# Second mixture's experts: plain scatters of half 1, the shared tiles moved behind all routed ones, and plain gathers into four pair buffers that VectorE adds to the rows

## The chip, the cores and the metric

The kernel runs on one core of one Trainium2 chip. The metric is the device time of one execution in microseconds (us), the median of several runs. Engines are called as in the profile: PE is TensorE, DVE VectorE, ACT ScalarE, POOL GpSimd, SP SyncE; SPq and POOLq are the DMA queues that SP and POOL fill.

## The reference, cut to what matters

Four layers run over 4096 rows of 128 numbers (16 sequences of 256): sparse attention, a mixture of experts, a state-space layer and a second mixture. The change lies in the last one:

```
scores = softmax(xf @ gate_w.T)
_, idx = top_k(scores + gate_b, 2)              # two of eight experts for each row
w      = take_along_axis(scores, idx)
expert(x, e) = silu((x@w1[e]+b1[e]) * (x@w3[e]+b3[e])) @ w2[e] + b2[e]
y = sum over the two chosen e of w * expert(x, e)
z = expert(x, shared)                            # every row also goes through a shared expert
out = x + y + z                                  # x: the rows that came in; y, z: of their normed copy
```

## The kernel before, in words

The 4096 rows are T = 32 tiles of 128 rows, in two halves of HT = 16 tiles. X (g_X in the profile) holds them in SBUF through all layers. For a mixture every row is sent to two slots, k = 0 and k = 1, of a buffer XG in HBM (rows in the profile), sorted by expert. Each half has NH = 39 tiles of slots, so NT = 78 routed tiles, and XG was zeroed at the program's start. POOL sends one tile of rows with one indirect DMA (`pool_scatter`, line 858); its argument op is ALU.bypass (a plain write) or ALU.add (the DMA reads the target, adds, writes). For each k the routing weight is first written beside the rows (`pool_reweight`, lines 846 to 854), which for k = 1 waits until the 16 scatters of k = 0 have landed. Half 0 of the second mixture is scattered by the state-space stage and by `dispatch` (lines 904 to 906, plain), half 1 by `experts` (lines 1106 to 1108, with add).

`experts` then runs one list of tiles, `sequence`, through a pipeline written out by hand. Each engine has a `step(s)` that handles tile s - lag: SP fetches tile s and stores tile s - 8; PE transposes tile s - 3 (m_x_TP, L1142), multiplies it up at s - 4 (m_x_UP, L1151), down at s - 6 (m_x_DP, L1171), and transposes the hidden values at s - 5 (m_x_HP, L1161); DVE adds the bias and multiplies the two parts at s - 4 (L1299, L1301) and takes the result at s - 6 (`output`); ACT copies out of PSUM between them. Routed tiles are fetched from XG (L1074), shared ones from the normed rows m_XS in SBUF (L1069). The list before has 110 places: routed tiles 0 to 38 (half 0), shared tiles 16 to 23, routed tiles 39 to 77 (half 1), shared tiles 0 to 15, shared tiles 24 to 31.

SP's fetch of a routed tile waits for `placed`, which POOL raises by 39 when a half's scatters have landed. A routed tile's result goes through m_x_YO to the HBM buffer Y (out_rows, L1079). When all stores of a half have landed, POOL gathers its rows back: 16 indirect DMAs for k = 0, a wait for their landing (`joined`), 16 for k = 1, each adding Y's rows into X (L1131). A shared tile i < 16 is added into X by DVE at once (L1324), after the gathers of its four tiles (`got[q]`). A shared tile i >= 16 is "late": DVE puts it into the buffer m_x_late (L1309), and after the pipeline four adds of 128x512 bring it into X (L1371), each behind the gathers of its four tiles. SP then stores X in eight pieces of 256 KB (L1096):

```
for h in range(2):
    for v in range(U):
        pool.wait_ge(stored[v], 16 * stores_of(v, (h + 1) * NH))
    for k in range(2):
        if k == 1:
            pool.wait_ge(joined, 16 * HT * (h + 1))
```

The first mixture runs through the same functions with `inside` true, no shared tiles and no `out`.

Of the kernel before, what the change touches and what calls it, by code (L numbers as in the profile page):

```python
# [17 lines left out]
P = 128  # L18
# [906 lines left out]
def experts(nc, tag, signals, d, inside, X, rt, XG, Y, out, n_early, w, gated, ident, ahead=None):  # L925
# [17 lines left out]
    sequence = [(False, i) for i in range(NH)]  # L943
    if n_shared:
        sequence += [(True, i) for i in range(HT, HT + LAG)]
    sequence += [(False, i) for i in range(NH, NT)]
    if n_shared:
        sequence += [(True, i) for i in range(HT)] + [(True, i) for i in range(HT + LAG, T)]
# [36 lines left out]
    with ExitStack() as ctx:  # L985
# [16 lines left out]
        late = m.sb("late", [P, HT * D]) if out is not None else None  # L1002
        W = 4
# [33 lines left out]
        with nc.Block() as block:  # L1037
# [63 lines left out]
            def _(pool):  # L1101
# [4 lines left out]
                for k in range(2):  # L1106
                    d.pool_reweight(pool, 1, k)
                    d.pool_scatter(pool, k, HT, T, ALU.add)
# [14 lines left out]
                else:  # L1123
                    for h in range(2):
                        for v in range(U):
                            pool.wait_ge(stored[v], 16 * stores_of(v, (h + 1) * NH))
                        for k in range(2):
                            if k == 1:
                                pool.wait_ge(joined, 16 * HT * (h + 1))
                            for t in range(h * HT, (h + 1) * HT):  # L1130
                                nc.gpsimd.indirect_dma_start(X[:, t * D:(t + 1) * D], None, Y[0:(h + 1) * NH * P, :],  # L1131
                                                             bass.IndirectOffsetOnAxis(rt.slot[k][:, t:t + 1], 0),
                                                             compute_op=ALU.add).then_inc(got[t % HT // W] if k else joined, 16)
# [151 lines left out]
            def _(dve):  # L1285
# [17 lines left out]
                def output(t, held):  # L1303
# [15 lines left out]
                    elif t.shared:  # L1319
                        nc.vector.tensor_tensor(YO[v][:], DP[v % 2][:, 0:D], w.b[:, ds(e + WU, D)], ALU.add).then_inc(y_summed.sem, 1)  # L1320
                        dve.wait_ge(y_summed.sem, y_summed.after(j))
                        dve.wait_ge(got[t.i // W], 16 * W)
# [42 lines left out]
                if out is not None:  # L1365
                    for q in range(HT // W):
                        t = HT + q * W
                        dve.wait_ge(got[q], 2 * 16 * W)
                        dve.wait_ge(y_summed.sem, y_summed.after(max(place_of_shared[i] for i in range(t, t + W))))
                        x = X[:, t * D:(t + W) * D]  # L1370
                        nc.vector.tensor_tensor(x, x, late[:, q * W * D:(q + 1) * W * D], ALU.add).then_inc(last_joined, 1)  # L1371
# [820 lines left out]
```

## Time and profile before

| | |
|---|---|
| median of 3 runs | 1232.14 us (1229.09 to 1233.37) |
| profiled execution, its own time | 1222.57 us |
| its span, first to last instruction | 1220.7 us |
| mean granted TensorE clock | 0.907 |
| busy in the span | PE 982.1 us (80%), DVE 946.0 (77%), POOL 835.1 (68%), ACT 741.5 (61%) |
| second mixture's experts | about 1014 us to the end |

The profiled execution is one run with the hardware profiler. Busy time is the time in which an engine had an instruction under way; a DMA issued by POOL is an instruction of POOL for as long as POOL works on it, and its data land later ("landing"). In a row of the timeline, the bracket tells how long the engine stood idle before the instruction, and what ended that.

### The profile page before, as it was taken

The page shows a single profiled execution, that of the slowest core. Times are in us where ns is not written, and L with a number is a line of the kernel's source. Part 1 is how long each engine was busy: PE and PEld are TensorE (multiplying, and loading weights), DVE is VectorE, ACT ScalarE, POOL GpSimd, SP SyncE. Part 2 cuts the span into 40 slices and gives each one's busy share as a digit, 9 for nine tenths or more (in the row PEclk, how much of TensorE's full clock was granted, in tenths as well). Part 3 has the DMA queues.
Part 4 walks back from the last instruction along what each step waited for, and adds up shares of the span by engine and source line. Part 5 has one row for each costly group of instructions (what it writes and reads, how often), then busy time and mean ns, then how long its engine had stood idle before and what let it go on. Part 6 is the DMA issues. An engine that isn't in the chain of part 4 may idle for free. (4 is left out here: it accounts for less than half of the span.)

```text
span 1220.7 us, 17047 instructions
## 1 busy us (share of the span) xinstructions
PE 982.1 (80%) x4202; PEld 596.9 (49%) x4202; DVE 946.0 (77%) x2295; ACT 741.5 (61%) x1656; POOL 835.1 (68%) x604
## 2 busy tenths in 40 slices
PE   5888868289999977788989988898857736999970
PEld 3666756268888842333333433342413224777750
DVE  6999999753333337799999999999999965777760
ACT  4867747165555557967686776667833215777740
POOL 3333339647527646788999988796949967767676
PEclk9999879589999988998999889999968867999995
DMA  9996002226525425253545353534335315756543
GB/s 271 158 156 179 1 8 20 35 50 92 83 69 92 86 37 125 95 156 124 164 146 173 128 164 102 174 122 138 125 102 151 107 41 90 123 103 122 106 94 65
DMA packets 140032, 133.50 MB, mean 109 GB/s; under 512 B 14578, under 2 KB 121186, under 8 KB 139810
## 3 DMA queue, kind: packets, MB, share of 16 engines
q1 hardware_dynamic: 107106, 115.55, 35.1%
q0 software_dynamic: 32832, 16.86, 12.3%
q8 instruction: 39, 0.64, 0.2%
q14 instruction: 55, 0.45, 0.1%
HBM read 98.66 MB, written 31.60 MB: 107 GB/s over the span
## 5 line engine op out<-in xcount | busy, mean ns | idle before, releaser
L1900 POOL TENSOR_TENSOR ss_HC<-ss_Hs,ss_Cb 128x512 f32<-128x512 f32 x256 | 330.3, 1460 | 75.0 <-DVE ss_Hs L1952 56.3
L1625 PE MATMUL ss_Y<-ss_HC,g_ident 128*128 128x512 f32 x512 | 269.3, 657 | 49.4 <-POOL ss_HC L1900 46.2
L1952 DVE TENSOR_TENSOR_SCAN ss_Hs<-ss_dA,ss_dBu 128x512 f32<-128x512 f32 x256 | 296.8, 1199 | 8.0 <-ACT ss_dA L1801 8.0
L1801 ACT ACTIVATE ss_dA<-ss_delta,g_A 128x510 f32<-128x510 f32 x256 | 168.9, 712 | 94.2 <-DVE ss_Hs L1952 94.0
L858 POOL DMA_INDIRECT rows<-m_XS,g_slot x128 | 178.8, 1397 | 60.3 <-issue 33.6
L1625 PEld LDWEIGHTS ss_Y<-ss_HC,g_ident 128*128 128x128 f32 x512 | 97.3, 205 | 203.1 <-POOL ss_HC L1900 131.6
L1151 PE MATMUL m_x_UP<-g_m_w,m_x_gT 128*128 (+1 forms) x532 | 192.4, 468 | 0.0
L1944 DVE TENSOR_TENSOR ss_dBu<-ss_duP,ss_Bb 128x512 f32<-128x512 f32 x256 | 163.0, 683 | 1.5 <-ACT ss_duP L1781 1.5
L1171 PEld LDWEIGHTS m_x_DP<-g_m_w,m_x_hT 128*128 128x128 f32 x908 | 121.8, 191 | 62.2 <-issue 34.5
L1171 PE MATMUL m_x_DP<-g_m_w,m_x_hT 128*128 (+1 forms) x908 | 140.8, 285 | 2.3 <-ACT m_x_hT L1243 2.3
L1243 ACT ACTIVATE m_x_hT<-m_x_HP 128x256 f32<-128x256 f32 (+1 forms) x188 | 80.4, 428 | 87.2 <-PE m_x_HP L1161 85.5
L1292 DVE SCALAR_TENSOR_TENSOR m_x_hid<-m_x_UP,m_x_G,m_x_sg 128x352 f32<-128x352 f32 x78 | 45.5, 583 | 110.3 <-ACT m_x_sg L1225 110.3
L1131 POOL DMA_INDIRECT g_X<-out_rows,g_slot x64 | 99.6, 1556 | 37.5 <-issue 18.3
L520 POOL TENSOR_TENSOR at_RP<-at_RP,a_rope 128x1024 f32<-128x1024 f32 x16 | 39.5, 2468 | 88.9 <-ACT at_RP L357 88.9
L1151 PEld LDWEIGHTS m_x_UP<-g_m_w,m_x_gT 128*128 128x128 f32 x532 | 87.8, 193 | 18.1 <-issue 1.7
L1299 DVE TENSOR_TENSOR m_x_sg<-m_x_UP,g_m_b 128x352 f32<-128x352 f32 x110 | 57.6, 524 | 32.5 <-PE m_x_UP L1151 32.2
L1161 PE MATMUL m_x_HP<-g_ident,m_x_hid 128*128 128x128 f32 x454 | 80.4, 273 | 2.5 <-DVE m_x_hid L1292 2.4
L1119 POOL DMA_INDIRECT g_X<-out_rows,g_slot x32 | 49.5, 1546 | 44.9 <-DMA out_rows<-m_x_YO 33.7
L1590 PE MATMUL ss_Q<-ss_xpad,ss_w_conv 128*128 128x512 f32 x128 | 60.6, 619 | 7.8 <-ACT ss_xpad L1730 7.8
L1142 PE MATMUL m_x_TP<-g_ident,m_x_G 128*128 128x128 f32 x188 | 52.3, 278 | 16.2 <-DMA m_x_G<-rows 15.0
L1225 ACT ACTIVATE m_x_sg<-m_x_UP 128x352 f32<-128x352 f32 x78 | 36.2, 464 | 39.9 <-PE m_x_UP L1151 39.9
L1161 PEld LDWEIGHTS m_x_HP<-g_ident,m_x_hid 128*128 128x128 f32 x454 | 55.9, 142 | 4.0 <-DVE m_x_hid L1292 2.6
(284 smaller groups left out, 1746.5 us busy)
## 6 DMA issues: line engine op xcount, KB each, us to landing
ss_Bb<-bc_rows SPq DMA_DIRECT2D x64, 512.0 KB, 4.6
ss_Cb<-bc_rows SPq DMA_DIRECT2D x64, 512.0 KB, 3.8
rows<-g_Z SPq DMA_DIRECT2D x2, 5031.0 KB, 53.4
m_x_G<-rows SPq DMA_DIRECT2D x156, 64.5 KB
out_rows<-m_x_YO SPq DMA_DIRECT2D x156, 64.0 KB
g_m_w<-in_w_up SPq DMA_DIRECT2D x1, 2816.0 KB, 11.3
g_m_b<-in_b SPq DMA_DIRECT2D x1, 2160.0 KB, 11.5
g_X<-in_x SPq DMA_DIRECT2D x4, 512.0 KB, 6.1
```

Of the source, the lines that this page charges most:

```text
L858: self.nc.gpsimd.indirect_dma_start(self.XG, bass.IndirectOffsetOnAxis(self.rt.slot[k][:, t:t + 1], 0), self.row(t), None, compute_op=op). ...
L1131: nc.gpsimd.indirect_dma_start(X[:, t * D:(t + 1) * D], None, Y[0:(h + 1) * NH * P, :], bass.IndirectOffsetOnAxis(rt.slot[k][:, t:t + 1], ...
L1151: ins = nc.tensor.matmul(UP[v % 2][:, at:at + n], gT[v % 2][:], w.w[:, ds(e + c, n)], start=True, stop=True)
L1161: ins = nc.tensor.transpose(HP[0:n, c * P:(c + 1) * P], hid[v % 2][:, c0:c0 + n], ident[:])
L1171: ins = nc.tensor.matmul(DP[v % 2][:, 0:D], hT[v % 2][0:n, c * P:(c + 1) * P], w.w[0:n, ds(e + WU + c * D, D)], start=c == 0, stop=c == NC ...
L1243: ins = nc.scalar.activation(hT[v % 2][:, 0:full], HP[:, 0:full], ACT.Copy)
L1590: ins = nc.tensor.matmul(dst, w_conv[:, h, k, :], xpad[:, h, :, k:k + S], start=k == 0, stop=k == K)
L1625: ins = nc.tensor.matmul(Yp[:, h, :], ident[:], HC[(c * N + n) % NHC][:, h, :], start=False, stop=n == N - 1)
L1801: nc.scalar.activation(dA[n % NA][:, h, :, 1:S], seqs(delta[v][:, h, :])[:, :, 1:S], ACT.Exp, scale=A[:, h, n:n + 1]).then_inc(dA_ready.se ...
L1900: nc.gpsimd.tensor_tensor(HC[(c * N + n) % NHC][:, h, :], Hs[n % 4][:, h, :], Cb[g % 2][:, n % 2, :], ALU.mult).then_inc(hc_ready.sem, 1)
L1944: v_.tensor_tensor(dBu[:, h, :], duP[:, h, :], Bb[g % 2][:, n % 2, :], ALU.mult).then_inc(dBu_ready.sem, 1)
L1952: v_.tensor_tensor_scan(Hs[n % 4][:, h, :], dA[n % NA][:, h, :, :].rearrange("p s t -> p (s t)"), dBu[:, h, :], 0.0, ALU.mult, ALU.add).th ...
```

## The change

Four things change, all in `experts` of the second mixture.

1. The scatters of half 1 are plain writes (ALU.bypass) there; the first mixture keeps ALU.add.
2. The list has all 78 routed tiles first, then the shared tiles 16 to 31, then the shared tiles 0 to 15.
3. The gathers no longer add into X. Each writes into one of four new SBUF buffers of 128 x 2048 numbers, `pair[h][k]` (m_x_pair in the profile), without a compute operation. The wait between k = 0 and k = 1 is gone; before half 1's gathers POOL waits until all of half 0's have landed.
4. DVE adds the buffers to X. For half 0, at every fourth of the shared tiles 0 to 15: pair[0][0] += pair[0][1], then X += pair[0][0], both 128x512 and chained by a semaphore. For half 1, behind the pipeline: four adds of m_x_late, four of pair[1][0], four of pair[1][1], each 128x512, with a chained wait between the groups; SP's last four stores wait for the last four adds.

```diff
-    sequence = [(False, i) for i in range(NH)]
+    sequence = [(False, i) for i in range(NT)]
     if n_shared:
-        sequence += [(True, i) for i in range(HT, HT + LAG)]
-    sequence += [(False, i) for i in range(NH, NT)]
-    if n_shared:
-        sequence += [(True, i) for i in range(HT)] + [(True, i) for i in range(HT + LAG, T)]
+        sequence += [(True, i) for i in range(HT, T)] + [(True, i) for i in range(HT)]
...
+        pair = [[m.sb(f"pair{h}{k}", [P, HT * D]) for k in range(2)] for h in range(2)] if out is not None else None
...
-                    d.pool_scatter(pool, k, HT, T, ALU.add)
+                    d.pool_scatter(pool, k, HT, T, ALU.add if inside else ALU.bypass)
...
+                        if h == 1:
+                            pool.wait_ge(joined, 16 * HT)
+                            for q in range(HT // W):
+                                pool.wait_ge(got[q], 16 * W)
                         for k in range(2):
-                            if k == 1:
-                                pool.wait_ge(joined, 16 * HT * (h + 1))
-                            for t in range(h * HT, (h + 1) * HT):
-                                nc.gpsimd.indirect_dma_start(X[:, t * D:(t + 1) * D], None, Y[0:(h + 1) * NH * P, :],
-                                                             bass.IndirectOffsetOnAxis(rt.slot[k][:, t:t + 1], 0),
-                                                             compute_op=ALU.add).then_inc(got[t % HT // W] if k else joined, 16)
+                            for t in range(HT):
+                                nc.gpsimd.indirect_dma_start(pair[h][k][:, t * D:(t + 1) * D], None, Y[0:(h + 1) * NH * P, :],
+                                                             bass.IndirectOffsetOnAxis(rt.slot[k][:, h * HT + t:h * HT + t + 1], 0),
+                                                             ).then_inc(got[t // W] if k else joined, 16)
...
-                        dve.wait_ge(got[t.i // W], 16 * W)
+                        q = t.i // W
+                        if t.i % W == 0:
+                            dve.wait_ge(joined, 16 * HT)
+                            dve.wait_ge(got[q], 16 * W)
+                            first, second = (pair[0][k][:, t.i * D:(t.i + W) * D] for k in range(2))
+                            link = Chain(dve, d.chain)
+                            link(nc.vector.tensor_tensor(first, first, second, ALU.add))
+                            x = X[:, t.i * D:(t.i + W) * D]
+                            link(nc.vector.tensor_tensor(x, x, first, ALU.add))
...
+                        x = X[:, t * D:(t + W) * D]
+                        dve.wait_ge(y_summed.sem, y_summed.after(max(place_of_shared[i] for i in range(t, t + W))))
+                        ins = nc.vector.tensor_tensor(x, x, late[:, q * W * D:(q + 1) * W * D], ALU.add)
+                    link = Chain(dve, d.chain)
+                    link(ins)
+                    dve.wait_ge(joined, 2 * 16 * HT)
+                    for q in range(HT // W):
+                        x = X[:, (HT + q * W) * D:(HT + (q + 1) * W) * D]
+                        ins = nc.vector.tensor_tensor(x, x, pair[1][0][:, q * W * D:(q + 1) * W * D], ALU.add)
+                    link(ins)
+                    for q in range(HT // W):
+                        x = X[:, (HT + q * W) * D:(HT + (q + 1) * W) * D]
                         dve.wait_ge(got[q], 2 * 16 * W)
-                        dve.wait_ge(y_summed.sem, y_summed.after(max(place_of_shared[i] for i in range(t, t + W))))
-                        x = X[:, t * D:(t + W) * D]
-                        nc.vector.tensor_tensor(x, x, late[:, q * W * D:(q + 1) * W * D], ALU.add).then_inc(last_joined, 1)
+                        nc.vector.tensor_tensor(x, x, pair[1][1][:, q * W * D:(q + 1) * W * D], ALU.add).then_inc(last_joined, 1)
```

The order on POOL, from the second mixture's gathers to the end, before (a row ends with the semaphores that it waits for; "x15" is fifteen such instructions; m1_x_stored0 to 3 count the stores to Y):

```order
L1131 DMA g_X<-out_rows,g_slot 128x128 [waits d_sent,m1_x_stored2,m1_x_stored3,m1_x_stored1,m1_x_stored0]
L1131 DMA g_X<-out_rows,g_slot 128x128 x15
L1131 DMA g_X<-out_rows,g_slot 128x128 [waits m1_x_joined]
L1131 DMA g_X<-out_rows,g_slot 128x128 x15
L1131 DMA g_X<-out_rows,g_slot 128x128 [waits m1_x_stored2,m1_x_stored3,m1_x_stored1,m1_x_stored0]
L1131 DMA g_X<-out_rows,g_slot 128x128 x15
L1131 DMA g_X<-out_rows,g_slot 128x128 [waits m1_x_joined]
L1131 DMA g_X<-out_rows,g_slot 128x128 x15
```

And after the change:

```order
L1131 DMA m_x_pair<-out_rows,g_slot 128x128 [waits d_sent,m1_x_stored2,m1_x_stored3,m1_x_stored1,m1_x_stored0]
L1131 DMA m_x_pair<-out_rows,g_slot 128x128 x31
L1131 DMA m_x_pair<-out_rows,g_slot 128x128 [waits m1_x_got0,m1_x_joined,m1_x_got1,m1_x_stored3,m1_x_got2,m1_x_stored2,m1_x_got3,m1_x_stored1,m1_x_stored0]
L1131 DMA m_x_pair<-out_rows,g_slot 128x128 x31
```

The 64 gathers are the same in number; the wait in the middle of each half is gone, and half 1 now also waits for half 0's landing.

The order on DVE at the end of the second mixture, the last places of the list and what follows, before:

```order
L1299 TENSOR_TENSOR m_x_sg<-m_x_UP,g_m_b 128x352 [waits t_silu_ready,t_up_ready]
L1301 TENSOR_TENSOR m_x_sg<-m_x_sg 128x176 [waits m1_x_biased]
L1309 TENSOR_TENSOR m_x_late<-m_x_DP,g_m_b 128x128 [waits t_down_ready] x3
L1371 TENSOR_TENSOR g_X<-g_X,m_x_late 128x512 [waits m1_x_y_summed,m1_x_got0]
L1371 TENSOR_TENSOR g_X<-g_X,m_x_late 128x512 [waits m1_x_y_summed,m1_x_got1]
L1371 TENSOR_TENSOR g_X<-g_X,m_x_late 128x512 [waits m1_x_y_summed,m1_x_got2]
L1371 TENSOR_TENSOR g_X<-g_X,m_x_late 128x512 [waits m1_x_y_summed,m1_x_got3]
```

The change, at its first of four such places (shared tile 0), and then at the very end:

```order
L1320 TENSOR_TENSOR m_x_YO<-m_x_DP,g_m_b 128x128 [waits m1_x_stored2,t_down_ready]
L1328 TENSOR_TENSOR m_x_pair<-m_x_pair 128x512 [waits m1_x_got0,m1_x_joined,m1_x_y_summed]
L1330 TENSOR_TENSOR g_X<-g_X,m_x_pair 128x512 [waits g_chain]
L1332 TENSOR_TENSOR g_X<-g_X,m_x_YO 128x128 [waits g_chain]
L1299 TENSOR_TENSOR m_x_sg<-m_x_UP,g_m_b 128x352 [waits t_silu_ready,t_up_ready]
```

```order
L1320 TENSOR_TENSOR m_x_YO<-m_x_DP,g_m_b 128x128 [waits m1_x_x_added,t_down_ready]
L1332 TENSOR_TENSOR g_X<-g_X,m_x_YO 128x128 [waits m1_x_y_summed]
L1378 TENSOR_TENSOR g_X<-g_X,m_x_late 128x512 [waits m1_x_y_summed] x4
L1384 TENSOR_TENSOR g_X<-g_X,m_x_pair 128x512 [waits m1_x_joined,g_chain]
L1384 TENSOR_TENSOR g_X<-g_X,m_x_pair 128x512 x3
L1389 TENSOR_TENSOR g_X<-g_X,m_x_pair 128x512 [waits m1_x_got0,g_chain]
L1389 TENSOR_TENSOR g_X<-g_X,m_x_pair 128x512 [waits m1_x_got1]
L1389 TENSOR_TENSOR g_X<-g_X,m_x_pair 128x512 [waits m1_x_got2]
L1389 TENSOR_TENSOR g_X<-g_X,m_x_pair 128x512 [waits m1_x_got3]
```

DVE has 16 adds of 128x512 more: eight among the shared tiles 0 to 15, in front of the next tile's L1299, and eight behind the last tile. None of them stands in front of the last tile's work in the same step.

## Rows read from the trace of the kernel before

**Rows 1.** The page's first line, and the chain of waits, 1176 us to the end (start, length, what).

```profile
span 1220.7 us, 17047 instructions
...
1181.75 3.16 DMA g_X<-out_rows,g_slot
...
1213.18 3.32 DMA g_X<-out_rows,g_slot
...
1216.52 0.69 DVE g_X L1371
```

**Rows 2.** Timeline of POOL, second mixture's scatters (start, length, engine, instruction, [idle before <-releaser]).

```profile
988.52 0.99 POOL L858 DMA_INDIRECT rows<-m_XS,g_slot  x1 [0.30 <-issue]
...
991.71 0.98 POOL L858 DMA_INDIRECT rows<-m_XS,g_slot  x1 [0.52 <-POOL m_XS L852]
...
1010.77 0.95 POOL L858 DMA_INDIRECT rows<-m_XS,g_slot  x1 [0.30 <-issue]
...
1015.34 1.59 POOL L858 DMA_INDIRECT rows<-m_XS,g_slot  x1 [0.52 <-POOL m_XS L852]
...
1076.15 1.55 POOL L858 DMA_INDIRECT rows<-m_XS,g_slot  x1 [0.30 <-issue]
```

**Rows 3.** Line 858 in 975 to 1012 us (plain), then in 1012 to 1080 us (add): ns min/median/max.

```profile
L858 POOL DMA_INDIRECT rows<-m_XS,g_slot x24: 954/958/1017, 975.4 to 1010.8; - x24
...
L858 POOL DMA_INDIRECT rows<-m_XS,g_slot x32: 1546/1546/1649, 1015.3 to 1076.2; - x32
```

**Rows 4.** Timeline of POOL: first gather of half 0, then k = 0 and 1 of half 1.

```profile
1083.81 1.55 POOL L1131 DMA_INDIRECT g_X<-out_rows,g_slot  x1 [6.11 <-DMA out_rows<-m_x_YO]
...
1153.76 1.54 POOL L1131 DMA_INDIRECT g_X<-out_rows,g_slot  x1 [8.81 <-DMA out_rows<-m_x_YO]
...
1185.17 1.54 POOL L1131 DMA_INDIRECT g_X<-out_rows,g_slot  x1 [1.88 <-DMA g_X<-out_rows,g_slot]
```

**Rows 5.** Busy time by stretch: engine busy us (x instructions), granted clock, DMA share, GB/s.

```profile
990.00:1010.00 20.00, 7.25 (x47) 6.25 (x46) 14.60 (x57) 3.98 (x6) 14.23 (x16) 0.59 0.15 50
1030.00:1040.00 10.00, 10.00 (x63) 7.08 (x61) 7.24 (x21) 7.91 (x34) 8.27 (x6) 1.00 0.87 129
...
1160.00:1170.00 10.00, 10.00 (x65) 7.50 (x63) 9.49 (x29) 5.69 (x23) 8.48 (x6) 1.00 0.49 86
...
1190.00:1200.00 10.00, 0.00 (x0) 0.00 (x0) 0.69 (x1) 0.00 (x0) 8.17 (x7) 0.50 0.37 59
```

**Rows 6.** Timeline of DVE: tiles of the shared part, and the last one's result.

```profile
1154.94 0.52 DVE L1299 TENSOR_TENSOR m_x_sg<-m_x_UP,g_m_b 128x352 f32<-128x352 f32 x1
...
1156.07 0.29 DVE L1324 TENSOR_TENSOR g_X<-g_X,m_x_YO 128x128 f32<-128x128 f32 x1
1156.28 0.52 DVE L1299 TENSOR_TENSOR m_x_sg<-m_x_UP,g_m_b 128x352 f32<-128x352 f32 x1
...
1168.87 0.53 DVE L1299 TENSOR_TENSOR m_x_sg<-m_x_UP,g_m_b 128x352 f32<-128x352 f32 x1
...
1169.69 0.28 DVE L1320 TENSOR_TENSOR m_x_YO<-m_x_DP,g_m_b 128x128 f32<-128x128 f32 x1
1170.01 0.29 DVE L1324 TENSOR_TENSOR g_X<-g_X,m_x_YO 128x128 f32<-128x128 f32 x1
1170.27 0.52 DVE L1299 TENSOR_TENSOR m_x_sg<-m_x_UP,g_m_b 128x352 f32<-128x352 f32 x1
...
1183.39 0.29 DVE L1309 TENSOR_TENSOR m_x_late<-m_x_DP,g_m_b 128x128 f32<-128x128 f32 x1 [1.11 <-PE m_x_DP L1171]
```

**Rows 7.** Groups of DVE by line in 1020 us to the end: busy us, mean ns of one.

```profile
L1324 DVE TENSOR_TENSOR g_X<-g_X,m_x_YO 128x128 f32<-128x128 f32 x16 | 4.7, 292 | 0.6
...
L1371 DVE TENSOR_TENSOR g_X<-g_X,m_x_late 128x512 f32<-128x512 f32 x4 | 2.8, 692 | 30.8 <-DMA g_X<-out_rows,g_slot 30.8
```

**Rows 8.** Timeline of SPq: the first fetch behind half 0's routed tiles (place 39).

```profile
1070.30 0.50 SPq L1069 DMA_DIRECT2D m_x_G<-m_XS  x1
```

**Rows 9.** DMA to landing of the eight stores of X (L1096): us min/median/max.

```profile
DMA to landing us min/median/max: 2.3/2.6/4.5
```

## The prediction

> **What bounds the kernel now.** I read the chain of waits first. In its last 37 us it holds POOL's gathers, their landing, one DVE add and nothing of PE [rows 1]: the last gather starts at 1213.18, lands 3.32 us later, DVE adds for 0.69 us, and 1220.7 - 1217.2 = 3.5 us go to the last store. The groups of DVE show the same from the other side: four adds of 128x512 waited 30.8 us for gathers [rows 7]. PE has nothing left after the last tile, whose result DVE takes at 1183.39 [rows 6]. So the last 33 us are POOL alone, and the end is set by two things: when half 1's stores have landed (the gathers start at 1153.76), and how fast POOL issues 32 gathers [rows 4]. Before 1153 us the bound is PE, busy all the time at full clock, and in the shared tiles 0 to 15 DVE is almost level with it, 9.49 of 10 us [rows 5].
>
> One thing in the timeline of POOL is the core of the case. Scatters on line 858 take 958 ns when plain and 1546 ns with add, with hardly any spread in either group [rows 3]. From start to start that is (1010.77 - 991.71) / 15 = 1.27 us against about 1.86 us, since 0.30 us of issue follow each [rows 2, 3]. The add gathers are like the add scatters, 1.54 us, also at the end when PE is idle and DVE all but idle [rows 4, 5]. So what costs is the add, not the direction and not the neighbours.
>
> **Step 1, plain scatters of half 1.** Start stays at 1015.34. Sixteen take 15 x 1.27 = 19.0 us to the last start; from there to the first of k = 1 the plain pair in the trace needs 991.71 - 988.52 = 3.2 us [rows 2]; again 19.0 us, the last instruction and about 2 us of landing: placed at 1015.3 + 19.0 + 3.2 + 19.0 + 3 = 1059.5. Before, the last scatter started at 1076.15. Nobody waits for this by itself: gain 0, but it is what pays step 2.
>
> **Step 2, the new order.** SP asks for place 39 at 1070.30 [rows 8]. That is now routed tile 39, which needs `placed`; 1059.5 is 11 us earlier, so PE does not stall. Of the 47 places between the last routed tile of half 0 and that of half 1, eight shared ones leave. The two starts of gathers are 1153.76 - 1083.81 = 69.95 us apart [rows 4]; a shared tile goes at 1.40 us (1168.87 to 1170.27 [rows 6]), so 69.95 - 8 x 1.40 = 58.75 us remain, and half 1's gathers can start at 1142.5, 11.2 us earlier. PE's total work is the same 110 tiles, so PE alone would still end about 1183.4. Half 0's gathers start at 1083.8 as before: stores of the same places.
>
> **Step 3, plain gathers.** No plain gather is in the trace. Bounds: the plain scatter, 0.96 us, and the add gather, 1.54 us (below 0.96 nothing suggests it; a gather has the same 128 rows). I take 0.96, 1.27 from start to start, since add scatter and add gather agree within 10 ns. Half 0 then ends issuing at 1083.8 + 31 x 1.27 = 1123.2 and lands by 1127, far from 1142.5, so the new wait for half 0's landing costs nothing; with 1.54 us (1.85 from start to start) it would land at 1145 and cost 3. Half 1: last start 1142.5 + 31 x 1.27 = 1181.9, landed at 1185.2 with the old 3.3 us. The dropped wait between k = 0 and k = 1 (1185.17 - 1181.75 - 1.85 = 1.6 us [rows 1, 4]) is in this count. POOL, the old bound, is ready 31 us earlier.
>
> **Step 4, DVE's adds.** This decides the end now. One add of 128x512 is 692 ns [rows 7]. (a) Eight of them sit among shared tiles 0 to 15, in four chained pairs: 2 x (0.69 + 0.035) = 1.45 us each time, 5.8 us (0.035 is what a chained wait adds: L1320 of 0.28 us at 1169.69, its dependent L1324 at 1170.01 [rows 6]). DVE needs 1.34 us for such a tile when it runs without a gap (1154.94 to 1156.28) and PE 1.40 [rows 6], so there is only 0.06 x 15 = 0.9 us of slack: the rest, 4.9 us, pushes PE. The bounds are 0 (the pipeline's two-deep buffers hide it) and 5.8. The last result, at 1183.4 before, comes at 1188.3; with its two short instructions it is done at 1188.9. (b) Behind it stand twelve adds. Independent ones overlap by 0.07 to 0.08 us (the 0.29 us L1324 at 1156.07, its successor at 1156.28 [rows 6]), so 0.62 each and two chained waits: 7.6 us, last add done at 1196.5. The gathers landed at 1185.2, so none of them waits for POOL. (c) The last four stores now come 0.6 us apart instead of 7.5; a store in a burst lands up to 4.5 us after its issue against 2.6 [rows 9]. I take 3.5 + 1.5 = 5 us: end at 1201.5.
>
> **The sum.** 1201.5 - 1220.7 = -19.2 us of span. Against the profiled execution's own time that is 1222.6 - 19.2 = 1203.4. The runs shown have their median 9.6 us above that execution; the change touches nothing that makes this gap, so the number for the median is 1232.1 - 19.2 = 1212.9, say **1213**. DMA load is no cost: a window with little but plain scatters keeps the 16 DMA engines 0.15 busy, one with add gathers alone 0.37 at a slower pace [rows 5].
>
> **Rivals.** *A: plain gathers cost POOL as much as adding ones.* For it: no row shows a plain gather, and reading scattered rows of HBM is another work than writing them. Against it: gather and scatter agree with add. Half 1 then starts at 1146, when half 0 has landed (1083.8 + 31 x 1.85 + 3.3 = 1144.5), the last lands at 1146 + 57.4 + 3.3 = 1206.7, and an add and a store follow: 1211, or -10: 1222. It decides from 1.25 us per gather on, where POOL's landing passes DVE's last group.
> *B: the adds of 4(a) are hidden.* DVE's delay at a result is absorbed by the slack that tiles have between engines: 4.9 us better, -24: 1208. Against it: DVE 9.49 of 10 busy.
> *C: DVE's adds and POOL's gathers hold each other up.* Each of the eight adds would stand until a gather is over, up to 0.96 us: +7.7 us, or -11.5: 1220.6. The rows are against it: L1324, with both inputs in SBUF, takes 292 ns while POOL issues gathers 8.48 of 10 us, as long as its size wants, and L1371 takes 692 ns each time [rows 5, 7]. The Trainium skill (SBUF — State Buffer, Who interferes with whom) says that a DVE instruction with two SBUF inputs contends with a GpSimd instruction that reads SBUF and the second to start fully blocks, but infers that descriptor generation needs only the write side; by the first half of that rule this rival holds, by the second it does not, and the trace agrees with the second.
> *D: the transfers of tiles come late.* This ends on the other side. Half 0's gathers now run at 1.27 instead of 1.86 us beside 39 routed tiles, each with a fetch and a store on the same DMA engines. If that pushes a fetch behind the moment when PE wants it, PE waits at every tile; from 0.5 us per tile on it eats the whole gain, and at 0.65 us x 39 = 25 us the time is 1238. Against it: with add scatters the DMA engines were 0.87 busy and PE still 10.00 of 10 [rows 5], and plain transfers load them less.
> *E: the clock.* With idle time PE's granted clock fell to 0.50 to 0.59 [rows 5]; if the waits of 4(a) do that for the 16 shared tiles, each takes up to 1.40 us more, +22.4, less the 4.9 that hide under it: -1.7, no change, 1230. The stretch would have PE over 80% busy, which speaks against it.
> *F: the scatters do not get cheaper beside running experts* (the plain rows are all from before them). Placed at about 1080 instead of 1070.3: PE stalls 10 us at place 39, -9: 1223.
>
> **How the numbers follow.** Forecast (gathers 0.96 us, adds pushing PE) 0.66; A 0.11; B 0.09; C 0.05; F 0.04; E 0.03; D 0.02. Its neighbours within 3 us on both sides cover the unknown of the store burst. From 1205 (B, less 3) to 1223 (A and C and F, just) all but E, D and tails lie inside, so low 1205, high 1223. About 0.3%, 3.7 us, is what a measurement of this kernel can tell from no change. Faster 0.94, same 0.035, slower 0.025.
>
> **What would show it.** The groups of the new profile: L858 in the second mixture all at about 958 ns; L1131 at about 958 (1540 is rival A). POOL's timeline: first gather of half 1 near 1142 (later than 1146: A, D or F). L1328 and L1330 at 690 ns (more: C). A PE m_x_UP that waits for DVE among the shared tiles, about 5 us in all (none: B), with the clock still at 0.9 or more (E). PE without a gap at 1075 (else F). The chain of waits should end DVE L1378, L1384, L1389 and a store, with no POOL in its last 10 us; POOL there makes the forecast wrong in its main step.

## The result and the profile after

The changed kernel takes **1324.8 us** (median of 4 runs, 1322.7 to 1330.5) against 1230.7 us for the kernel before in the same session: a ratio of 1.078, 95% interval 1.0749 to 1.0811. It is 94 us slower. The forecast was 1213 us, range 1205 to 1223.

The profiled execution took 1322.7 us. Its page begins as follows (busy time, then parts of the view in 40 slices of 33 us):

```profile
span 1320.8 us, 17051 instructions
## 1 busy us (share of the span) xinstructions
PE 1004.5 (76%) x4202; PEld 609.7 (46%) x4202; DVE 958.6 (73%) x2311; ACT 742.5 (56%) x1656; POOL 777.4 (59%) x604
...
PE   5887966599999777898999789895752469359355
...
PEclk9999888699999898899999898996885679779778
```

PE's busy time grew by 22 us only, the span by 100. In the last nine slices, in which the experts' tiles run, PE stands at 3 to 6 tenths in three separate pairs of slices; in the kernel before the routed tiles keep it at 9.

POOL did what was forecast. These are the lines of its source view that answer to [rows 3], first for the scatters of half 1, then for the gathers (duration min/median/max in ns, first and last start), and the starts of both gather blocks, which answer to [rows 4]:

```profile
L858 POOL DMA_INDIRECT rows<-m_XS,g_slot x32: 954/958/979, 1020.8 to 1062.1; - x32
```

```profile
L1131 POOL DMA_INDIRECT m_x_pair<-out_rows,g_slot x64: 940/944/1074, 1124.7 to 1262.4; - x64
```

```profile
1124.72 0.98 POOL L1131 DMA_INDIRECT m_x_pair<-out_rows,g_slot  x1 [61.68 <-DMA out_rows<-m_x_YO]
...
1223.68 0.94 POOL L1131 DMA_INDIRECT m_x_pair<-out_rows,g_slot  x1 [59.14 <-DMA out_rows<-m_x_YO]
```

Plain scatters of 0.96 us beside running experts, plain gathers of 0.94 us, and half 1 scattered by 1065. But POOL then stands idle for 61.7 and 59.1 us, until Y is complete: the first gather of half 0 starts at 1124.7, that of half 1 at 1223.7.

The windows of the new kernel show where the tiles stay (columns as in [rows 5]: PE, PEld, DVE, ACT and POOL busy, granted clock, DMA share, GB/s):

```profile
1030.00:1050.00 20.00, 4.98 (x18) 2.99 (x18) 2.32 (x6) 1.82 (x8) 13.83 (x16) 0.61 0.21 62
1090.00:1110.00 20.00, 20.00 (x123) 14.57 (x123) 14.43 (x41) 16.29 (x69) 0.00 (x0) 1.00 0.35 93
1150.00:1170.00 20.00, 2.27 (x6) 0.79 (x4) 1.16 (x3) 0.66 (x3) 11.18 (x12) 0.50 0.18 50
1200.00:1220.00 20.00, 19.97 (x122) 14.32 (x121) 14.56 (x42) 15.41 (x63) 0.00 (x0) 1.00 0.32 90
1240.00:1260.00 20.00, 3.28 (x9) 1.87 (x9) 1.32 (x4) 0.90 (x3) 15.13 (x17) 0.50 0.19 56
```

Without POOL's DMAs PE is as dense as before: 123 matmuls in 20 us, at full clock. In the three stretches in which POOL issues plain indirect DMAs it gets 18, 6 and 9, at a granted clock of 0.50 to 0.61. All engines are nearly idle there, and the 16 DMA engines too (0.18 to 0.21). The three bills can be read from three dates. They are counted from PE's first routed tile, since that one comes 5.4 us later in this execution, for what lies ahead of the changed code:

```profile
1022.11 0.45 PE L1142 MATMUL m_x_TP<-g_ident,m_x_G 128*128 128x128 f32 x1 [12.68 <-DMA m_x_G<-rows]
```

In the execution of before it was

```profile
1016.72 0.45 PE L1142 MATMUL m_x_TP<-g_ident,m_x_G 128*128 128x128 f32 x1 [12.95 <-DMA m_x_G<-rows]
```

By that clock the forecast had half 0's gathers at 67.1 us, half 1's at 125.8 and the end at 184.8; they came at 102.6, 201.6 and 298.7, so 35.5, 75.8 and 113.9 us late. Each block of 32 plain indirect DMAs, which takes POOL 32 x 1.26 = 40 us, costs the tiles 35 to 40 us. They all but stop while it is issued.

What they wait for is odd. This is the view of waits (engine and tile, what ended the wait, us in total, times, longest):

```profile
PEld m_x_DP L1171 <- issue: 121.2, 86, 17.6
...
ACT m_x_hT L1243 <- remote: 103.0, 9, 17.6
```

"issue" is a wait for nothing that the profile shows, "remote" one that it can put down to no instruction or queue that it knows. The kernel before has 34.5 us of it in the first group, its longest 0.9:

```profile
PEld m_x_DP L1171 <- issue: 34.5, 79, 0.9
```

### The profile page after: what moved, and what is told of

The parts are those of the page before. It is cut to its first block and busy times, and to the rows that moved or that the text cites. A ratio compares the mean times of both kernels' runs of the same rounds, so it can differ in the third digit from the quotient of the medians.

```text
span 1320.8 us, 17051 instructions
## 1 busy us (share of the span) xinstructions
PE 1004.5 (76%) x4202; PEld 609.7 (46%) x4202; DVE 958.6 (73%) x2311; ACT 742.5 (56%) x1656; POOL 777.4 (59%) x604
## 5 line engine op out<-in xcount | busy, mean ns | idle before, releaser
L1171 PE MATMUL m_x_DP<-g_m_w,m_x_hT 128*128 (+1 forms) x908 | 146.2, 292 | 96.5 <-ACT m_x_hT L1243 54.7
L1171 PEld LDWEIGHTS m_x_DP<-g_m_w,m_x_hT 128*128 128x128 f32 x908 | 127.4, 198 | 160.8 <-issue 121.2
L1151 PE MATMUL m_x_UP<-g_m_w,m_x_gT 128*128 (+1 forms) x532 | 198.8, 481 | 0.1
L858 POOL DMA_INDIRECT rows<-m_XS,g_slot x128 | 160.2, 1251 | 59.6 <-issue 34.9
L1131 POOL DMA_INDIRECT m_x_pair<-out_rows,g_slot x64 | 60.6, 946 | 139.7 <-DMA out_rows<-m_x_YO 120.8
L1299 DVE TENSOR_TENSOR m_x_sg<-m_x_UP,g_m_b 128x352 f32<-128x352 f32 x110 | 57.5, 523 | 97.6 <-PE m_x_UP L1151 50.4
L1161 PE MATMUL m_x_HP<-g_ident,m_x_hid 128*128 128x128 f32 x454 | 83.8, 282 | 6.0 <-ACT m_x_hid L1230 3.6
L1117 POOL DMA_INDIRECT g_X<-out_rows,g_slot x32 | 49.3, 1542 | 43.9 <-DMA out_rows<-m_x_YO 32.6
L1142 PE MATMUL m_x_TP<-g_ident,m_x_G 128*128 128x128 f32 x188 | 54.1, 288 | 18.9 <-DMA m_x_G<-rows 12.7
```

What stands on the lines that cost most here:

```text
L858: self.nc.gpsimd.indirect_dma_start(self.XG, bass.IndirectOffsetOnAxis(self.rt.slot[k][:, t:t + 1], 0), self.row(t), None, compute_op=op). ...
L1142: nc.tensor.transpose(TP[:, 0:P], G[v][:, 0:D], ident[:]).then_inc(turned.sem, 1)
L1151: ins = nc.tensor.matmul(UP[v % 2][:, at:at + n], gT[v % 2][:], w.w[:, ds(e + c, n)], start=True, stop=True)
L1161: ins = nc.tensor.transpose(HP[0:n, c * P:(c + 1) * P], hid[v % 2][:, c0:c0 + n], ident[:])
L1171: ins = nc.tensor.matmul(DP[v % 2][:, 0:D], hT[v % 2][0:n, c * P:(c + 1) * P], w.w[0:n, ds(e + WU + c * D, D)], start=c == 0, stop=c == NC ...
L1299: nc.vector.tensor_tensor(sg[v % 2][:], UP[v % 2][:, 0:WU], w.b[:, ds(e, WU)], ALU.add).then_inc(biased.sem, 1)
```

## The experiments

Three theories stood at the start. **P**: plain indirect DMAs, issued back to back, hold up what goes through PE. **The order**: the 78 routed tiles in a row, or DVE's new adds, cost the time. **Rival D** of the prediction: transfers of tiles come late. Theory P was refined twice below.

**1. Plain scatters alone**, in the kernel before.

```diff
-                    d.pool_scatter(pool, k, HT, T, ALU.add)
+                    d.pool_scatter(pool, k, HT, T, ALU.add if inside else ALU.bypass)
```

> The kernel before, with nothing but the 32 scatters of half 1 of the second mixture made plain. Theory P (while POOL issues plain indirect DMAs beside the running tile pipeline, everything that waits for PE is served late): in the changed kernel half 0's stores were done 35 us later than in the kernel before, counted from the first scatter, so this kernel is about 35 us slower than before, near 1265, with waits of 5 to 14 us behind PE in the first 45 us of the experts and none later. Rival O (the new order of the list, or SP's queue behind it, starves the pipeline): no change, within 2 us of before, or a little faster. Rival B (the pair buffers and DVE's adds): no change.

Measured: 1264.7 us, ratio 1.031 (1.026 to 1.035). One word in the program costs 37 us. The window in the middle of the scatters, which in the kernel before holds 124 matmuls:

```profile
1030.00:1050.00 20.00, 7.93 (x36) 5.53 (x34) 4.25 (x11) 3.77 (x16) 13.80 (x16) 0.74 0.24 69
```

The next, from the kernel before:

```profile
1030.00:1050.00 20.00, 20.00 (x124) 14.51 (x123) 14.40 (x41) 15.82 (x67) 14.22 (x10) 1.00 0.80 124
```

The busier DMA engines (0.80, adding scatters) do no harm, the idler ones (0.24) do. And in the changed kernel PE waits for a fetched tile once, for the very first (12.7 us, 13.0 before): rival D is out.

**2. The new order alone**, in the kernel before.

```diff
-    sequence = [(False, i) for i in range(NH)]
+    sequence = [(False, i) for i in range(NT)]
...
-        sequence += [(True, i) for i in range(HT, HT + LAG)]
-    sequence += [(False, i) for i in range(NH, NT)]
-    if n_shared:
-        sequence += [(True, i) for i in range(HT)] + [(True, i) for i in range(HT + LAG, T)]
+        sequence += [(True, i) for i in range(HT, T)] + [(True, i) for i in range(HT)]
```

> The kernel before, with nothing but the new order of the list; scatters and gathers keep their add. Theory P: no long waits behind PE anywhere; the add scatters are placed near 1080 and place 39 is wanted at 1070, so PE stalls about 10 us there, half 1's stores come 11 us earlier and are given back: within 5 us of before. Rival O: most of the 94 us is here, 1290 or more.

Measured: 1230.1 us, ratio 1.0026 (1.0008 to 1.0043), 2.5 us more: the order costs nothing to speak of. With adding scatters PE now waits for the first routed tile of half 1, the stall that step 2 named for unpaid placement:

```profile
1087.14 0.48 PE L1139 MATMUL m_x_TP<-g_ident,m_x_G 128*128 128x128 f32 x1 [4.79 <-DMA m_x_G<-rows]
```

**3. The change with adding scatters**, so that only the gathers are plain.

```diff
-                    d.pool_scatter(pool, k, HT, T, ALU.add if inside else ALU.bypass)
+                    d.pool_scatter(pool, k, HT, T, ALU.add)
```

> The changed kernel with the scatters of half 1 adding again, all else kept. Theory P: the first episode (35 us) goes, a stall of about 10 us at place 39 comes, the episodes beside the two sets of 32 plain gathers stay (about 40 us each): near 1295 to 1300. Rival O or B: the time stays at 1325 or, if the scatter matters to the order, rises.

Measured: 1296.2 us, ratio 1.056 (1.052 to 1.061). Two of the three held stretches are left, and 69 of the 94 us, among them a stall of 5.6 us at half 1's first routed tile, which with adding scatters isn't placed in time.

**4. The change, paced.** Behind each plain indirect DMA of the second mixture POOL writes a scratch tile of 512 columns and waits for it. Everything else is the change.

```diff
+        def pause(pool, k):
+            nc.gpsimd.memset(rest[:], 0.0).then_inc(d.s.reweighted.sem, 1)
+            d.s.reweighted.base += 1
+            pool.wait_ge(d.s.reweighted.sem, d.s.reweighted.after(1, k + 1))
...
-                    d.pool_scatter(pool, k, HT, T, ALU.add if inside else ALU.bypass)
+                    for t in range(HT, T):
+                        d.pool_scatter(pool, k, t, t + 1, ALU.add if inside else ALU.bypass)
+                        if not inside:
+                            pause(pool, k)
...
                                                              ).then_inc(got[t // W] if k else joined, 16)
+                                pause(pool, 1)
```

> The changed kernel with a POOL memset of 128x512 and a wait for it behind each of the 96 plain indirect DMAs, so that they start 1.9 to 2.0 us apart, slower than the adding ones (1.86). Theory P in the form 'pace' (the plain ones hurt because they follow each other in 1.26 us and leave a gap of 0.3): the long waits go or shrink to a quarter, the time falls to 1240 or below. Theory P in the form 'kind' (each plain one holds PE up for as long as it is worked on, 0.95 us): the episodes last longer (1.55 times) with the pipeline a little quicker in them, 1310 to 1340. Rival O: 1325 as before.

Measured: **1219.9 us**, ratio 0.995 (0.991 to 0.998). 96 added instructions and 96 added waits make the changed kernel 105 us faster. The timeline of POOL, and the windows of this kernel:

```profile
1024.36 0.97 POOL L858 DMA_INDIRECT rows<-m_XS,g_slot  x1 [0.28 <-POOL m_x_rest L1004]
1025.32 0.54 POOL L1004 MEMSET m_x_rest<- 128x512 f32 x1
1026.14 0.97 POOL L858 DMA_INDIRECT rows<-m_XS,g_slot  x1 [0.28 <-POOL m_x_rest L1004]
```

```profile
1030.00:1050.00 20.00, 20.00 (x123) 14.71 (x122) 14.41 (x40) 15.93 (x65) 16.94 (x23) 1.00 0.51 121
...
1130.00:1150.00 20.00, 19.96 (x124) 14.60 (x124) 14.73 (x42) 15.24 (x61) 16.52 (x22) 1.00 0.48 129
```

The same DMAs in the same places, 1.78 us apart instead of 1.26, and PE has no gap. So the pace is what counts, not that they are plain.

**5 and 6. Shorter pauses**: the scratch tile cut to 1 column, and to 192.

```diff
-        rest = m.sb("rest", [P, 512])
+        rest = m.sb("rest", [P, 1])
```

> plain_paced with the memset behind each plain indirect DMA cut from 512 columns to 1, so that a plain indirect DMA starts about every 1.35 to 1.45 us instead of 1.78 (paced) or 1.26 (the change). Theory P (the pace of the plain DMAs alone sets whether the handovers behind TensorE get late): if the limit lies above 1.45 us the episodes return nearly whole and the time is 1270 to 1325; if it lies below, the time is 1208 to 1215, under plain_paced's 1219.9 because the gathers of half 1 take 0.35 us less each. Theory S (what helps is that POOL waits for its own semaphore between DMAs, whatever the time): 1208 to 1215 too, with the pace still at 1.4. The start-to-start time in the POOL timeline tells P and S apart only if the episodes return.

Measured: 1315.2 us, ratio 1.067 (1.062 to 1.072), one DMA each 1.35 us. The wait for a semaphore of its own is still there and doesn't help. (The paces given are those of the scatters; the gathers come 1.33 us apart here, 1.50 in the next and 1.77 in experiment 4.)

> plain_paced with a memset of 192 columns, a plain indirect DMA every 1.5 to 1.6 us. Theory P: between pause_tiny and plain_paced; if pause_tiny shows episodes, this one tells whether they shrink by degrees with the pace (a time half-way, 1240 to 1280) or vanish at once (1212 to 1218). Theory S: 1212 to 1218, in line with the pace of the last gathers.

Measured: 1271.9 us, ratio 1.032 (1.027 to 1.037), one DMA each 1.52 us. The held stretches don't vanish at a threshold, they fade: in the middle of half 0's gathers PE issues 17 matmuls in 20 us at 1.35 us, 54 at 1.52, and 124 at 1.78.

```profile
1130.00:1150.00 20.00, 4.79 (x17) 3.76 (x18) 1.45 (x4) 2.34 (x10) 15.92 (x31) 0.59 0.22 61
```

```profile
1130.00:1150.00 20.00, 10.32 (x54) 6.51 (x54) 6.96 (x18) 7.34 (x30) 16.47 (x27) 1.00 0.34 88
```

**7. What exactly is late.** Until here the lateness could lie in the semaphores that PE raises, in its matmuls, or in something of the tile pipeline. Behind the last store of the changed kernel come six short phases: its output is complete by then, and the total time means nothing.

```diff
+                    for p in range(PHASES):
+                        if p:
+                            pe.wait_ge(joined, 16 * (2 * HT + 32 * (p - 1)))
...
+                        pe.wait_ge(t_copied.sem, copied(p))
+                        if p < 3:
+                            for i in range(128):
+                                ins = nc.tensor.matmul(TP[:, 0:P], ident[:], ident[:], start=True, stop=True)
+                                if p == 2 or i == 127:
+                                    ins.then_inc(turned.sem, 1)
+                        elif p != 4:
+                            for i in range(40):
+                                pe.wait_ge(t_copied.sem, copied(p) + i)
+                                nc.tensor.matmul(TP[:, 0:P], ident[:], ident[:], start=True, stop=True).then_inc(turned.sem, 1)
```

> The changed kernel with six short phases put behind its last store: 0: TensorE runs one row of 128 matmuls of its own operands alone; 1: the same beside 32 plain gathers issued back to back; 2: the same with a semaphore increment by each matmul; 3: 40 steps of TensorE matmul and ScalarE copy, each waiting for the other, beside 32 plain gathers; 4: 40 steps of ScalarE and VectorE copies that wait for one another, TensorE idle, beside 32 plain gathers; 5: phase 3 beside 32 adding gathers. Theory I (TensorE's increments of semaphores get late, the matmuls themselves do not): phase 1 takes as long as phase 0, phase 3 takes several times as long per step as phase 5, phase 4 is prompt. Theory M (the matmuls themselves or their reading get late): phase 1 is far longer than phase 0. Theory X (something of the tile pipeline is needed, its many HWDGE transfers or its weight of traffic): phases 1 to 5 all prompt, as in the dispatch stage before the change. Total about 1325 plus 250 to 500 us.

Measured, phase 0 and the beginning of phase 1, in PE's timeline (the profile shows each of these matmuls as two):

```profile
1325.76 30.83 PE L1229 MATMUL m_x_TP<-g_ident 128*128 128x128 f32 x256 [11.45 <-DMA out<-g_X]
1357.05 9.67 PE L1229 MATMUL m_x_TP<-g_ident 128*128 128x128 f32 x84 [0.46 <-ACT m_x_gT L1321]
1367.84 0.60 PE L1229 MATMUL m_x_TP<-g_ident 128*128 128x128 f32 x3 [1.13 <-issue]
```

and near the end of phase 2:

```profile
1456.01 0.37 PE L1229 MATMUL m_x_TP<-g_ident 128*128 128x128 f32 x1 [2.43 <-issue]
1458.81 0.37 PE L1229 MATMUL m_x_TP<-g_ident 128*128 128x128 f32 x1 [2.43 <-issue]
```

This settles it against semaphores (theory I), against a part of the tile pipeline (theory X) and for theory M. These matmuls wait for nothing, read one constant tile and write one place; alone they run without a gap, 0.12 us for each row of the profile. Beside plain gathers 84 rows go through in 9.7 us, and then they come late, in the end one every 2.8 us, with one weight load half-way between two (at 1454.61, 1457.41 and 1460.21), so that PE gets one instruction every 1.4 us; it is free again 6.4 us after the last gather was started. The 40 steps between PE and ACT of phase 3 were prompt for 19 us (0.9 to 1.2 us each) and then took 2.7 to 5.6 us until the gathers were over; beside adding gathers (phase 5) all 40 took 1.2. The 40 steps between ACT and DVE in phase 4 (0.6 us each, over in 24 us) were never held. That says less than it seems, because in this phase POOL itself stopped for 3.4 us behind its 17th gather, 21 us into the phase, and started again when the steps were nearly over:

```profile
1572.87 0.95 POOL L1149 DMA_INDIRECT m_x_pair<-out_rows,g_slot  x1 [3.36 <-issue]
```

**8. Which engines, and what of the DMAs counts.** Seven phases in the same place: other engines in a dense row, wide matmuls, a pause, and gathers of half the rows.

```diff
+                            rows = P // 2 if p == 5 else P
...
+                    for i in range(256):
+                        ins = nc.vector.tensor_copy(late[:, 8 * i:8 * i + 8], ident[:, 0:8])
...
+                            for i in range(256):
+                                nc.scalar.activation(late[:, 8 * i:8 * i + 8], ident[:, 0:8], ACT.Copy).then_inc(t_copied.sem, 1)
...
+                        for i in range(40 if p == 3 else 128):
+                            ins = nc.tensor.matmul(TP[:, 0:(4 if p == 3 else 1) * P], ident[:], X[:, 0:(4 if p == 3 else 1) * P], start=True, stop=True)
```

> The changed kernel with seven short phases behind its last store, each of them but the first beside 32 gathers. 0: 128 matmuls of TensorE alone. 1: 256 copies of 8 columns by VectorE beside plain gathers, back to back. 2: the same by ScalarE. 3: 40 matmuls of 512 columns by TensorE. 4: 128 matmuls of 128 columns beside plain gathers 1.78 us apart. 5: beside plain gathers of 64 rows instead of 128, back to back. 6: beside adding gathers, back to back. Theory E (TensorE alone gets its instructions late, whatever their size): phases 1 and 2 run without a gap, phase 3 shows gaps from about 10 to 18 us behind the first gather, 4 and 6 none. Theory A (any engine that issues densely gets them late): gaps of 0.7 us and more in phases 1 and 2 too. Phase 5 tells rows from DMAs: gaps if the number of DMAs or their pace counts (they then start every 0.9 to 1.3 us), none or fewer if the rows and the bytes count.

Measured: theory E fell. VectorE in phase 1 (its timeline; the gathers run from 1352.1 on):

```profile
1351.90 5.44 DVE L1441 COPY m_x_late<-g_ident 128x8 f32<-128x8 f32 x71 [34.50 <-ACT m_x_gT L1330]
1357.82 0.68 DVE L1441 COPY m_x_late<-g_ident 128x8 f32<-128x8 f32 x8 [0.48 <-issue]
...
1392.50 0.17 DVE L1441 COPY m_x_late<-g_ident 128x8 f32<-128x8 f32 x1 [1.23 <-issue]
1393.90 0.17 DVE L1441 COPY m_x_late<-g_ident 128x8 f32<-128x8 f32 x1 [1.23 <-issue]
...
1397.40 8.67 DVE L1441 COPY m_x_late<-g_ident 128x8 f32<-128x8 f32 x117 [0.46 <-issue]
```

71 copies of 0.08 us, then mostly one or two each 0.7 or 1.4 us, and full speed again from 1397.4, 6.5 us after the last gather was started at 1390.9. ScalarE in phase 2 does the same (68 copies in 6.8 us before the first gap, and 130 without one from 1451.9 on):

```profile
1406.45 6.80 ACT L1324 ACTIVATE m_x_late<-g_ident 128x8 f32<-128x8 f32 x68
```

So it is not a matter of PE: **each of the three engines, when it runs many instructions in a row, is held up**, in the depth of the hold to one instruction every 1.4 us. The view by stretch of phases 3 to 6 (wide matmuls; paced gathers; gathers of 64 rows; adding gathers):

```profile
1465.00:1503.00 38.00, 35.87 (x79) 15.63 (x80) 0.00 (x0) 0.00 (x0) 28.83 (x31) 0.96 0.19 50
1511.00:1542.00 31.00, 31.00 (x256) 30.93 (x256) 0.00 (x0) 0.00 (x0) 25.20 (x34) 0.92 0.14 37
1572.00:1614.00 42.00, 16.57 (x91) 15.19 (x90) 0.00 (x0) 0.00 (x0) 28.79 (x32) 0.62 0.10 25
1638.00:1667.00 29.00, 28.82 (x256) 28.66 (x256) 0.00 (x0) 0.02 (x1) 24.18 (x16) 1.00 0.29 35
```

With wide matmuls, of four times the columns, PE works 36 us before its first gap, and the gathers are then nearly over. But this gap comes behind 79 of the phase's 80 rows:

```profile
1464.91 36.00 PE L1235 MATMUL m_x_TP<-g_X,g_ident 128*128 128x512 f32 x79 [113.35 <-ACT m_x_late L1324]
1503.12 0.59 PE L1235 MATMUL m_x_TP<-g_X,g_ident 128*128 128x512 f32 x1 [2.21 <-issue]
```

Narrow ones were first held behind 84 and 79 rows (phases 1 and 2 of experiment 7, after 9.7 and 9.3 us) and 73 (phase 5 here, after 11.3 us). So in a dense row of PE the hold begins after a number of instructions, not after a time, and whether a longer row of wide ones would have been held like the narrow ones was not seen. With gathers 1.8 us apart, plain or adding, PE has no gap in 256 rows. Gathers of 64 rows, started 1.21 us apart, hold PE like those of 128, though they move 25 GB/s where the harmless adding ones move 35. Neither bytes nor DMA load count here, but how often POOL starts one.

**9 and 10. The change with pauses only where they are needed.** In both the last eight gathers follow each other at once, since by then PE is nearly or quite done; in the second the scratch tile also has 384 columns.

```diff
-                                pause(pool, 1)
+                                if not (h == 1 and k == 1 and t >= 8):
+                                    pause(pool, 1)
```

> plain_paced without the pause behind the last eight gathers, which start when TensorE's last matmul is done: 8 times (1.78 - 1.26) = 4.2 us less at the end, 1215 to 1217, and no episode since nothing on TensorE is left to be late. If the late handovers also hit VectorE's adds and the stores (which wait for DMAs and not for TensorE), 1220 or more.

Measured: 1216.8 us, ratio 0.988 (0.984 to 0.992).

> paced_until_done with the memset cut from 512 to 384 columns, a plain indirect DMA every 1.65 to 1.68 us instead of 1.78. By pe_bench and pause_mid (1.52 us: TensorE still held up, 1271.9 us) the limit lies between 1.52 and 1.78. If it lies under 1.65: no wait of ScalarE on TensorE of over 3 us, and the 24 paced gathers of half 1 before the last eight take 24 times 0.12 = 2.9 us less: 1213 to 1215. If it lies above: 1225 to 1250, with such waits back.

Measured: **1215.1 us** (6 runs against 11 of before), ratio 0.985 (0.983 to 0.988; not clear of experiment 9), one DMA each 1.67 us, and PE dense in the middle of half 0's gathers:

```profile
1130.00:1150.00 20.00, 19.97 (x122) 14.41 (x122) 14.50 (x40) 15.94 (x67) 16.74 (x25) 1.00 0.50 131
```

It has the lowest time of all, 18 us under the kernel before, and meets the forecast's dates, counted from the first routed tile: the gathers of half 1 start 126.4 us behind it (forecast 125.8), the span ends 184.6 us behind it (forecast 184.8). The pauses no longer cost time at the end: DVE's last four adds start at 1207.0 behind the others without a wait, where in experiments 4 and 9 the last one waited 6.5 and 2.4 us for gathers. The first tile, and the first gather of half 1:

```profile
1029.50 0.45 PE L1154 MATMUL m_x_TP<-g_ident,m_x_G 128*128 128x128 f32 x1 [12.58 <-DMA m_x_G<-rows]
```

```profile
1155.85 0.95 POOL L1141 DMA_INDIRECT m_x_pair<-out_rows,g_slot  x1 [5.43 <-DMA out_rows<-m_x_YO]
```

## Why the prediction was wrong

The step that failed is one that the prediction priced at nothing, in two sentences: "Nobody waits for this by itself: gain 0" (step 1), and "DMA load is no cost" under the sum. Both looked at what the DMAs load, POOL and the DMA engines. The runs show a cost of 35 to 40 us for each of three blocks of 32, on something that neither view has a column for: the instructions of the other engines. Steps 1 and 3 each carried it unpriced. Experiments 1 and 3 measured them apart; 4 took the cost from both and left the rest.

The rest, point by point:

- *Step 1.* The duration is right (0.96 us, 1.26 from start to start), the last scatter starts at 1062.1. Rival F fell: scatters do get cheaper beside experts.
- *Step 2.* The order alone costs 2.5 us (experiment 2), with a stall of 4.8 us where nothing makes the placement earlier; in the changed kernel PE has none there. Its forecast gain of 11.2 us is hidden in the change by the held stretches, and is there in the last experiment, 10.7 us: 137.0 us from the first tile to the gathers of half 1 before, 126.4 now.
- *Step 3.* A plain gather takes 0.94 us, 0.96 was assumed. Rival A fell.
- *Step 4 (a).* Four shared tiles with their two adds take 6.8 us (chain below) against 4 x 1.40 = 5.6: 1.2 us a group, which for four groups is the 4.9 forecast. Rival B fell. The changed kernel doesn't test rival C, since half 1's gathers are over before these adds begin. Experiments 4, 9 and 10 do, and it fell: there all eight adds run while POOL issues gathers, and each takes 691 to 693 ns, as before. In the last experiment for instance:

```profile
1189.41 1.07 POOL L1141 DMA_INDIRECT m_x_pair<-out_rows,g_slot  x1 [0.27 <-POOL m_x_rest L1004]
```

```profile
1189.89 0.69 DVE L1340 TENSOR_TENSOR m_x_pair<-m_x_pair 128x512 f32<-128x512 f32 x1
```

- *Step 4 (b), (c).* The twelve adds go from 1309.6 to 1317.2, 7.6 us as forecast. From there to the end it is 3.6 us, where 5 were assumed.

The chain of waits of the changed kernel, near its end:

```profile
1290.76 0.70 DVE m_x_pair L1328
...
1297.56 0.70 DVE m_x_pair L1328
...
1304.41 0.70 DVE m_x_pair L1328
...
1309.60 2.50 DVE g_X L1378 x4
1312.73 1.90 DVE g_X L1384 x3
1314.66 0.69 DVE g_X L1389
```

- *Rival D* had the sign and the place (tiles beside plain DMAs), but a wrong cause and 25 us where 114 were lost: with adding scatters the DMA engines are busier and PE is dense. *Rival E*, the clock, came with the hold, and not with the adds that it was about: 0.50 to 0.61 in the three held stretches, where PE has little to do, and 1.00 between them. What it adds to them was not measured by itself.

Could the trace of before have shown it? Its plain scatters stand where the other engines do little: in the first line of [rows 5] PE and DVE issue 47 and 57 instructions in 20 us. The prediction took from there that plain ones disturb nobody. But that row only says so for engines that ask for little; in the second line PE alone asks for 63 matmuls in 10 us. So the cost of plain DMAs beside a dense engine was an unknown without a row, and should have been given a wide upper bound, as the prediction did for the duration and not for the neighbours.

The mechanism stays open. How instructions reach the engines was not itself tried. The Trainium skill (Runtime: NRT & Kernel Launch, Instruction fetch mechanics) says that each engine fetches its instructions by a DMA queue of its own, in blocks of 256, and that the cost of crossing from one block to the next is mostly hidden. The lateness here does not come in such blocks: they soon come singly, in steps of 0.7 us or a multiple. In the 60 us around phase 2 of experiment 7 the DMA view has a single transfer of instructions:

```profile
q8 instruction: 1, 0.02, 0.1%
```

A late block alone therefore doesn't explain it. That a dense row shows 68 to 84 rows of the profile before its first gap, whether they last 5.4 us or 36, looks like a stock that is used up, but this is a reading, not a measurement, and the steps of phase 3 in experiment 7 were held after 40 rows of PE already. Whether adding DMAs would hold the engines too if POOL could start them faster is open as well, since it can't. So is the part of the recording: every execution on record, timed or profiled, comes with its span and granted clock, which suggests that instructions were being recorded in all of them, and no run tells whether that takes part in the hold.

## What to carry to other kernels

An instruction made cheaper on an engine off the critical path raises that engine's rate, and the rate can be the cost: look for a row in which it already runs at that rate beside neighbours as dense as those it will meet, and where there is none, leave the upper bound open. When long waits end in "issue" or "remote", the profile names nothing that is late; put a pause into the suspected neighbour before looking for a dependency. Here 0.4 us behind each plain indirect DMA but the last eight saved 110 us.

## What the runs showed of the hardware

- Plain indirect DMAs from POOL (128 rows) take it 0.94 to 0.96 us, adding ones 1.54, scatter or gather alike, beside dense engines too.
- Started every 1.21 to 1.35 us, they hold up the instructions of PE, DVE and ACT; at 1.50 to 1.52 us in part; at 1.67 us and above not visibly.
- The hold begins behind 68 to 84 rows of the profile of a dense row (5.4 to 11.3 us with short instructions, 36 us with matmuls of 512 columns), after 19 us in a row of steps between PE and ACT, and ends 5 to 7 us after the last DMA was started. In its depth PE, DVE and ACT get one instruction every 1.4 us each, a weight load counted as one.
- DVE's adds of 128x512 with both inputs in SBUF take 691 to 693 ns beside plain gathers too.
- Half the rows in each DMA change nothing in this, and spare POOL little: 0.90 instead of 0.94 us.
